# Squares of two layernorms moved from VectorE to ScalarE, with three other steps placed later

## The chip, the cores and the metric

One NeuronCore of a Trainium2 chip runs the whole program. The metric is the device time of one execution, in microseconds (us); lower is better.

## The reference, cut to what matters

```python
x = conv(x)                      # 8 x 56 x 56 x 64: 32 paths of 1x1, 3x3, 1x1 convs, summed, + x, relu
t = tokens(x)                    # 8 images of 3136 tokens, 64 channels
t = t + mamba(_ln_t(t))          # forward and backward selective scan, 128 channels, 16 states
t = t + ffn(_ln_t(t))            # 8 experts of 256, the best two of each token, mixed

def _ln_t(v, eps=1e-05):
    m = jnp.mean(v, axis=-1, keepdims=True)
    s = jnp.var(v, axis=-1, keepdims=True)
    return (v - m) / jnp.sqrt(s + eps)
```

The first lines are a summary; the mamba and the experts begin with a layernorm of their own. The kernel works in float32, or in bfloat16 parts that add up to it.

## The kernel before, in words

An image is cut in 7 chunks of 448 tokens (`CH`), each 4 tiles of 112 (`KT`, `TT`). The scan of one image takes 14 steps, one for each chunk and direction, with 16 slots each: 224 slots (`G`). In a slot `n`, TensorE picks the products for it (`pick_du`, L686, three matmuls into one of three banks), VectorE multiplies them by B (`weigh_b`, L1011, one slot ahead) and scans (`scan`, L1021), ScalarE makes the decays up to six slots ahead (`dA`, L864, in place in `dtb`, which a DMA spreads from DRAM), GpSimd multiplies by C (`by_c`, L1184), and TensorE gathers the result (L698). `pick_du` of slot n waits for the scan of slot n - 3.

Everything else is laid into these slots beside the scan. Stage A makes the next image's chunks: the convs, the first layernorm and its transposes. Stage E takes the finished chunks through the second layernorm, the router and the experts. Tables give each step its slot, relative to a chunk's start: `A_AT` (L62) and `E_AT` (L66). A chunk of A and one of E come every 32 slots, so the pattern repeats 56 times. Each engine has a loop over the slots and issues in order what the tables say. What follows counts slots within the 32, from the start of a chunk of E.

- **Norms.** `norm_mean` (L1058) sums the channels (L1059) and subtracts the mean (L1060, into `t[:, 0]`); `norm_var` (L1062) squares (L1063) and sums (L1064); `norm_pow` (L1066) divides by C (L1067), adds epsilon (L1068) and does three more small operations. All of it is on VectorE, each operation waiting for the one ahead. GpSimd raises to the power -1/2 (`power`, L1227; the operation is L1229) and writes the scaled tokens, twice. The first norm (tile `tmp`) is in slots 23 (mean) and 24 (the rest), the second (tile `tmpd`) in slots 0 and 1.
- **Ring.** Transposes and matmuls of A and E (`ring_job`) take two banks in turn; each waits until the bank's last content has been taken by ScalarE (`take`) or VectorE. The experts' first matmuls (`up`, L750) come in two bursts, two in each of the slots 24 to 27 and 0 to 3, and ScalarE takes them with Gelu (L906). `norm_T` (L739), `pair` (L760), `second` (L726, taken into h2p at L885) and `third` (L733) are ring jobs too.
- **Shared bank.** `misc_job` uses one bank for B (`bb`, L770), C (`cc`, L772), the next step's x and dt, and the tokens' transposes (`tokens_T`, L785). Each waits until the one ahead has been taken: B by `copy_bb` (L937), C by `copy_cc` (L943).
- **Mixing.** `down` (L821) gives a pair of experts, and `pair_out` (L1108) multiplies it on VectorE by the weights that ScalarE has put in `wb`, in slots 28, 31, 4 and 7. `wb` is the same tile as `rz`, into which ScalarE takes eight of the sixteen products of the convs' third stage (L895) from slot 8 on.
- **dt.** GpSimd makes dt (`soft_dt`, L1206) in slot 3 of a step; SP writes it (L537) and spreads it back over the partitions (L545).

Of the kernel before, what the change touches and what calls it, by code (L numbers as in the profile page):

```python
# [61 lines left out]
A_AT = {"cut": -16, "second": -11, "put0": -10, "rem1": -10, "split1": -7, "put1": -6, "rem2": -8,  # L62
        "split2": -5, "put2": -4, "arrange": -4, "z": 6, "x_in": 6, "paths": 14, "mean": 15, "var": 16,
        "power": 16, "scaled": 17, "normed": 18, "norm_T": 22, "keep_xn": 24}
F_AT = {"fetch": -4, "x_T": 0, "paths_in": 2, "rows": 4}
E_AT = {"mean": 0, "var": 1, "power": 2, "normed": 3, "tokens_T": 7, "logits": 10, "compare": 11, "places": 13,  # L66
        "lead": 13, "ask": 15, "weigh": 17, "share": 19, "weights": 20, "weight_parts": 21, "parts": 26,
# [13 lines left out]
def build(nc, T):  # L81
    ctx = ExitStack()
    with ctx:
# [5 lines left out]
        def sem(name):  # L89
            s = ctx.enter_context(nc.semaphore(name))  # L90
            sems.append(s)
            return s
# [275 lines left out]
        for s in sems:  # L368
# [11 lines left out]
            ("bu_ps", "bu_ok", "a_ok", "h_ok", "st_ok", "hc_ok", "y_acc", "gated", "o_ps", "o_rd", "st0"))  # L380
        v_ch, pw_req, pd_req = sem("v_ch"), sem("pw_req"), sem("pd_req")
        xa_in, rs_in = [sem("xa_in0"), sem("xa_in1")], [sem("rs_in0"), sem("rs_in1")]
        slab_in, h3_in, bounced = sem("slab_in"), sem("h3_in"), sem("bounced")
# [26 lines left out]
        def emit(p, run, a_imgs, e_imgs):  # L410
# [93 lines left out]
            for k in range(STEPS):  # L504
                if second_half(k):
                    MISC += [(DS * k + 4, "bb", k + 1), (DS * k + 5, "cc", k + 1)]
                if first_half(k):
                    MISC += [(DS * k + 12, "x", k + 2), (DS * k + 15, "dt", k + 2)]
# [23 lines left out]
            with nc.Block() as block:  # L532
# [318 lines left out]
                def _(act):  # L851
# [19 lines left out]
                    def take(what, of):  # L871
# [15 lines left out]
                        elif what == "third":  # L887
# [5 lines left out]
                            if m < 4:  # L893
                                after(ye_dve, earlier("E", "down", slots["A", "third", of]))
                            last = A.activation(rz[:, m % 4, :], out[:, 0:CH], ACT.Relu, bias=bnb[:, 2 + j:3 + j])  # L895
# [53 lines left out]
                    def keep_tokens(it):  # L949
                        act.wait_ge(m_ps, misc_made("tokens_T", it))  # L950
                        after(r_ps, made("up", (back(it, 2), MT - 1)))
                        A.activation(xn2[:, side(it), :], ps[MB][:, 0:CH], ACT.Copy).then_inc(m_act, 1)

                    def weigh(it):
                        act.wait_ge(e_req, upto("E", "ask", it))
                        A.activation(l1[:, 4, :], l1[:, 3, :], ACT.Exp).then_inc(e_ok, 1)  # L956
# [3 lines left out]
                    for n in range(SLOTS):  # L960
# [17 lines left out]
                        for a in (1, 2):  # L978
                            for it in now("A", ("", "split1", "split2")[a], n):
                                split_h2(it, a)  # L980
                        for it in now("E", "weigh", n):
                            weigh(it)
                        if k < STEPS:
                            if i == 5 and second_half(k):
                                copy_bb(k + 1)
                            if i == 6 and second_half(k):
                                copy_cc(k + 1)
                            if i == 15 and first_half(k):
                                soft_in(k + 2)

                @block.vector
                def _(dve):
# [64 lines left out]

                    def norm_mean(src, st, t):  # L1058
                        link(V.reduce_sum(st[:, 0, :], src, axis=AX.X))  # L1059
                        link(V.scalar_tensor_tensor(t[:, 0], bc_last(st[:, 0, :], C), -1.0 / C, src, ALU.mult, ALU.add))  # L1060

                    def norm_var(st, t):  # L1062
                        link(V.tensor_tensor(t[:, 1], t[:, 0], t[:, 0], ALU.mult))  # L1063
                        link(V.reduce_sum(st[:, 1, :], t[:, 1], axis=AX.X))  # L1064

                    def norm_pow(st, q, asked):  # L1066
                        link(V.tensor_scalar(st[:, 2, :], st[:, 1, :], 1.0 / C, None, ALU.mult))  # L1067
                        link(V.tensor_scalar(q[:, 0, 0, :], st[:, 2, :], LN_EPS, None, ALU.add))  # L1068
                        link(V.reciprocal(st[:, 3, :], q[:, 0, 0, :]))
                        link(V.tensor_tensor(st[:, 4, :], st[:, 2, :], st[:, 3, :], ALU.mult))  # L1070
                        V.tensor_scalar(q[:, 0, 1, :], st[:, 4, :], LN_EPS, None, ALU.add).then_inc(asked, 1)

                    def tokens_in(it):
# [3 lines left out]
                        after(d_tok, upto("E", "normed", back(it)))  # L1077
                        norm_mean(res_of(it, c), statd, tmpd)

# [42 lines left out]
                    for n in range(SLOTS):  # L1122
# [14 lines left out]
                        for it in now("A", "mean", n):  # L1137
                            norm_mean(res_of(it, A_ORD[it[1]]), stat, tmp)
                        for it in now("A", "var", n):
                            norm_var(stat, tmp)  # L1140
                            norm_pow(stat, pw, pw_req)
# [4 lines left out]
                        for it in now("E", "var", n):  # L1146
                            norm_var(statd, tmpd)
                            norm_pow(statd, pwd, pd_req)
# [264 lines left out]
```

## Time and profile before

| | |
|---|---|
| median of 3 runs | 5355.45 us (5351.28 to 5372.19) |
| the profiled execution | 5343.31 us |
| its span, first to last instruction | 5341.4 us |
| TensorE, VectorE, ScalarE, GpSimd busy | 83%, 78%, 62%, 74% |
| mean granted TensorE clock | 0.922 |

Busy time is the sum of the instructions on an engine. The ends of matmuls are modelled. "Waits" say for whom an engine stood idle and for how long; in the names, `ps` is a bank, and L numbers are lines of the kernel. PE is TensorE, DVE VectorE, ACT ScalarE and POOL GpSimd.

### The profile page before, as it was taken

To read this page: it belongs to the slowest core of one execution; us is meant where nothing else is said; L and a number is where in the kernel's file an instruction comes from. 1 tells how busy PE (TensorE), PEld (TensorE's weight loads), DVE (VectorE), ACT (ScalarE), POOL (GpSimd) and SP (SyncE) were. 2 spreads that over 40 slices of the span, in tenths; PEclk is the share of its full clock that TensorE was granted. 3 is DMA by queue.
4 is the path that set the end of the run, shared out by engine and by line. 5 is a ranking of instruction groups with operands and counts; after the bars stand their busy time and mean duration, and the time that the engine had idled before them with its cause. 6 is when DMAs were issued, how large, how long until landed. Compare 5 with 4: busy or idle time off the path is not lost. (4 is left out here: it accounts for less than half of the span.)

```text
span 5341.4 us, 71012 instructions
## 1 busy us (share of the span) xinstructions
PE 4435.6 (83%) x21206; PEld 1807.8 (34%) x21206; DVE 4141.3 (78%) x6297; ACT 3305.9 (62%) x5293; POOL 3949.6 (74%) x4937
## 2 busy tenths in 40 slices
PE   3577788888888888888888888788888888888887
PEld 1223333333333333333333333333333333332332
DVE  2278888788878887888878888788878888788871
ACT  1255466666666666666666666666666667666665
POOL 1267787778877877887878788778777778788872
PEclk9588899999999998999999999899999999999997
DMA  2365655555545554555555555455555555454420
GB/s 69 69 140 140 139 131 116 126 123 129 123 118 128 124 130 108 132 132 122 128 117 133 123 126 127 112 122 127 121 115 125 130 120 131 112 118 112 97 67 5
DMA packets 255561, 623.36 MB, mean 117 GB/s; under 512 B 105268, under 2 KB 170676, under 8 KB 255028
## 3 DMA queue, kind: packets, MB, share of 16 engines
q1 hardware_dynamic: 255156, 618.60, 50.2%
q8 instruction: 176, 2.88, 0.2%
q14 instruction: 229, 1.88, 0.1%
HBM read 540.85 MB, written 77.65 MB: 116 GB/s over the span
## 5 line engine op out<-in xcount | busy, mean ns | idle before, releaser
L1184 POOL TENSOR_TENSOR hc<-hs,cb 128x448 f32<-128x448 f32 x1792 | 2045.7, 1144 | 839.1 <-DVE hs L1021 810.3
L1021 DVE TENSOR_TENSOR_SCAN hs<-dtb,state,ps 128x448 f32<-128x448 f32 x1792 | 2049.0, 1143 | 110.2 <-DVE ps L1011 3.4
L1011 DVE TENSOR_TENSOR ps<-ps,bb 128x448 f32<-128x448 f32 x1792 | 1099.4, 614 | 508.8 <-PE ps L686 507.5
L686 PE MATMUL ps<-dux,pick 128*128 128x448 bf16 x3584 | 1066.3, 380 | 162.0 <-DVE hs L1021 99.7
L864 ACT ACTIVATE dtb<-dtb,decay 128x448 f32<-128x448 f32 x1792 | 1091.3, 658 | 95.7 <-DMA dtb<-dt_scratch 94.1
L906 ACT ACTIVATE hg<-ps,be 128x448 f32<-128x448 f32 x896 | 520.1, 631 | 576.9 <-PE ps L750 576.7
L686 PE MATMUL ps<-duz,pick 128*128 128x448 bf16 x1792 | 660.5, 369 | 0.0
L750 PE MATMUL ps<-xn,we 64*128 64x448 f32 x1792 | 578.2, 619 | 45.1 <-ACT hg L906 43.6
L895 ACT ACTIVATE rz<-ps,bnb 128x448 f32<-128x448 f32 x448 | 281.3, 628 | 476.3 <-DVE yw L1108 256.7
L686 PEld LDWEIGHTS ps<-dux,pick 128*128 128x128 bf16 x3584 | 273.1, 101 | 862.2 <-issue 444.3
L733 PE MATMUL ps<-h,w 96*128 96x448 bf16 x896 | 313.7, 385 | 219.6 <-ACT rz L895 82.3
L698 PE MATMUL ps<-hc,gather 128*32 128x448 f32 x3584 | 460.2, 587 | 5.4 <-POOL hc L1184 5.0
L821 PE MATMUL ps<-hg,we 128*64 128x448 f32 x1792 | 413.6, 585 | 18.0 <-ACT rz L913 7.0
L1044 DVE SCALAR_TENSOR_TENSOR acc<-ps,nb,acc 128x448 f32<-128x448 f32 x392 | 266.1, 679 | 189.3 <-PE ps L733 189.2
L810 PE MATMUL ps<-ident,rz 128*112 128x128 f32 x1792 | 297.2, 293 | 0.0
L975 ACT ACT_TABLE_LOAD x225 | 288.7, 1283 | 4.0
L750 PEld LDWEIGHTS ps<-xn,we 64*128 64x128 f32 x1792 | 199.4, 193 | 268.0 <-ACT hg L906 164.3
L810 PEld LDWEIGHTS ps<-ident,rz 128*112 128x112 f32 x1792 | 226.9, 142 | 157.6 <-issue 132.9
L686 PEld LDWEIGHTS ps<-duz,pick 128*128 128x128 bf16 x1792 | 179.1, 100 | 201.5 <-issue 34.2
L1282 POOL TENSOR_TENSOR yw<-yw 128x448 f32<-128x448 f32 x168 | 190.8, 1136 | 68.0 <-DVE yw L1108 68.0
L1225 POOL TENSOR_TENSOR h<-h,h2p 128x448 f32<-128x448 f32 x112 | 116.2, 1038 | 162.2 <-ACT h2p L885 104.3
L733 PEld LDWEIGHTS ps<-h,w 96*128 96x128 bf16 x896 | 84.0, 100 | 438.3 <-ACT rz L895 142.3
(177 smaller groups left out, 6426.5 us busy)
## 6 DMA issues: line engine op xcount, KB each, us to landing
dtb<-dt_scratch SPq DMA_DIRECT2D x448, 896.0 KB, 6.6
slab<-h_scratch SPq DMA_DIRECT2D x168, 290.0 KB, 8.1
dt_scratch<-sp SPq DMA_DIRECT2D x112, 224.0 KB, 2.0
h_scratch<-h2p SPq DMA_DIRECT2D x168, 112.0 KB
h<-h_scratch SPq DMA_DIRECT2D x56, 336.0 KB, 4.2
h_scratch<-h1s SPq DMA_DIRECT2D x56, 232.0 KB, 3.7
xw<-xn_scratch SPq DMA_DIRECT2D x112, 112.8 KB, 2.7
xw<-xn_scratch SPq DMA_DIRECT2D x112, 112.5 KB, 2.7
```

The source lines that it names most:

```text
L686: last = MM(ps[BU[n % 3]][:, 0:CH], pick[:, i, :], part, start=(a == 0), stop=(a == 2))
L698: last = MM(ps[YB][32 * q:32 * q + 32, 0:CH], gather[:, 24 - 8 * j:56 - 8 * j], hc[:, (4 * b + q) % 8, :], start=False, stop=(j == 3), ski ...
L733: last = MM(out[:, 0:CH], w3[:, j // 2, 2 * (j % 2):2 * (j % 2) + 2, :].rearrange("p a b -> p (a b)"), h3[:, j // 2, :], start=True, stop= ...
L750: last = MM(out[:, 0:CH], we1[half, m, :], xn2[half, side(it), :], start=True, stop=True)
L810: last = MM(ps[AB][0:TT, j * 128:(j + 1) * 128], src[:, j * TT:(j + 1) * TT], ident[:, :], is_transpose=True, start=(m == 0 and j == 0), s ...
L821: last = MM(ps[AB][C * h:C * h + C, 0:CH], we2[:, ORDER[g], :], hg[:, g % 8, :], start=(g % 4 < 2), stop=(g % 4 >= 2))
L864: A.activation(a, a, ACT.Exp, scale=decay[k % 2][:, i:i + 1]).then_inc(a_ok, 1)
L906: last = A.activation(hg[:, g % 8, :], out[:, 0:CH], ACT.Gelu, bias=be1[:, m:m + 1])
L975: A.preload_act_table_set("natural_log_exp_and_others")
L1011: V.tensor_tensor(bank, bank, bb[:, k % 2, :], ALU.mult).then_inc(bu_ok, 1)
L1021: V.tensor_tensor_scan(rev(hs[:, n % RH, :], d), rev(dtb[i // 4][:, i % 4, :], d), rev(bank, d), state[:, d, i:i + 1], ALU.mult, ALU.add). ...
L1184: P_.tensor_tensor(hc[:, n % 8, :], hs[:, n % RH, :], cb[:, k % 2, :], ALU.mult).then_inc(hc_ok, 1)
```

## The change

The square of both norms is computed by ScalarE (`square`), with the function Square and scale C^-0.5, so that the sum of the squares is the variance; the division by C is gone. VectorE signals the centred tokens (`x_mid`, `d_mid`), no longer waits for its own write of them, and waits for the squares (`x_sq`, `d_sq`) instead. The steps behind the mean come one slot later: variance, power, scaled, normed, `norm_T` and `keep_xn` of A; variance, power, normed and `tokens_T` of E. The product for C and its copy come one slot later. And a Relu of the third stage into `rz` no longer waits for all four pairs: the first waits for the first pair, the second for the second, and so on.

```diff
-        "split2": -5, "put2": -4, "arrange": -4, "z": 6, "x_in": 6, "paths": 14, "mean": 15, "var": 16,
-        "power": 16, "scaled": 17, "normed": 18, "norm_T": 22, "keep_xn": 24}
+        "split2": -5, "put2": -4, "arrange": -4, "z": 6, "x_in": 6, "paths": 14, "mean": 15, "square": 17, "var": 17,
+        "power": 17, "scaled": 18, "normed": 19, "norm_T": 23, "keep_xn": 25}
...
-E_AT = {"mean": 0, "var": 1, "power": 2, "normed": 3, "tokens_T": 7, "logits": 10, "compare": 11, "places": 13,
+E_AT = {"mean": 0, "square": 2, "var": 2, "power": 3, "normed": 4, "tokens_T": 8, "logits": 10, "compare": 11, "places": 13,
...
-                    MISC += [(DS * k + 4, "bb", k + 1), (DS * k + 5, "cc", k + 1)]
+                    MISC += [(DS * k + 4, "bb", k + 1), (DS * k + 6, "cc", k + 1)]
...
-                                after(ye_dve, earlier("E", "down", slots["A", "third", of]))
+                                after(ye_dve, earlier("E", "down", slots["A", "third", of]) - 3 + m)
...
+                    def square(t, centred, squared, count):
+                        act.wait_ge(centred, count)
+                        A.activation(t[:, 1], t[:, 0], ACT.Square, scale=C ** -0.5).then_inc(squared, 1)
...
+                        for it in now("A", "square", n):
+                            square(tmp, x_mid, x_sq, upto("A", "mean", it))
+                        for it in now("E", "square", n):
+                            square(tmpd, d_mid, d_sq, upto("E", "mean", it))
...
-                            if i == 6 and second_half(k):
+                            if i == 7 and second_half(k):
                                 copy_cc(k + 1)
...
-                    def norm_mean(src, st, t):
+                    def norm_mean(src, st, t, centred):
                         link(V.reduce_sum(st[:, 0, :], src, axis=AX.X))
-                        link(V.scalar_tensor_tensor(t[:, 0], bc_last(st[:, 0, :], C), -1.0 / C, src, ALU.mult, ALU.add))
-
-                    def norm_var(st, t):
-                        link(V.tensor_tensor(t[:, 1], t[:, 0], t[:, 0], ALU.mult))
-                        link(V.reduce_sum(st[:, 1, :], t[:, 1], axis=AX.X))
+                        V.scalar_tensor_tensor(t[:, 0], bc_last(st[:, 0, :], C), -1.0 / C, src, ALU.mult, ALU.add)\
+                            .then_inc(centred, 1)
+
+                    def norm_var(st, t, squared, count):
+                        dve.wait_ge(squared, count)
+                        link(V.reduce_sum(st[:, 2, :], t[:, 1], axis=AX.X))
...
-                        link(V.tensor_scalar(st[:, 2, :], st[:, 1, :], 1.0 / C, None, ALU.mult))
```

In the orders of the built programs, the lines of the changed kernel are one to nine higher than those above, by place. On ScalarE, at the burst of slots 0 to 3 (`hg` are the Gelus, `xns` the first norm's output, `sp` the steps of dt, `h2p` a split of the convs' second stage), before:

```order
L898 ACTIVATE xns<-ps,gb 128x448
L913 ACTIVATE rz<-ps 128x448
L926 ACTIVATE sp<-ps,dvec 128x448
L927 ACTIVATE sp<-ps,dvec 128x448
L929 ACTIVATE sp<-sp 128x448
L931 ACTIVATE sp<-sp 128x448
L906 ACT_TABLE_LOAD
L906 ACTIVATE hg<-ps,be 128x448 x4
L947 ACTIVATE h2p<-h 128x448
L906 ACTIVATE hg<-ps,be 128x448 x4
L975 ACT_TABLE_LOAD
```

and with the change, from the same place on:

```order
L927 ACTIVATE sp<-ps,dvec 128x448
L928 ACTIVATE sp<-ps,dvec 128x448
L930 ACTIVATE sp<-sp 128x448
L932 ACTIVATE sp<-sp 128x448
L899 ACTIVATE xns<-ps,gb 128x448
L907 ACT_TABLE_LOAD
L907 ACTIVATE hg<-ps,be 128x448 x4
L948 ACTIVATE h2p<-h 128x448
L907 ACTIVATE hg<-ps,be 128x448 x2
L957 ACTIVATE tmpd<-tmpd 112x256
L907 ACTIVATE hg<-ps,be 128x448 x2
L980 ACT_TABLE_LOAD
```

`xns` is now taken right ahead of the burst, and the Square (`tmpd<-tmpd`) stands behind the sixth of the eight Gelus; no table load comes with it, here or at the first norm, where it stands behind the fourth.

On TensorE from slot 5 on (`wcc` is the product for C, `wT,pick_w` a pair's weights, `pick` the products of a slot, `wo` the output projection, `xntd` the tokens' transposes, `hg,we` the experts' second matmul), before:

```order
L686 MATMUL ps<-duz,pick 128x448
L772 MATMUL ps<-u,wcc 128x448
L760 MATMUL ps<-wT,pick_w 128x448
L686 MATMUL ps<-dux,pick 128x448 x2
L686 MATMUL ps<-duz,pick 128x448
L705 MATMUL ps<-wo,zy 112x64 x4
L686 MATMUL ps<-dux,pick 128x448 x2
L686 MATMUL ps<-duz,pick 128x448
L785 MATMUL ps<-ident,xntd 128x112 x4
L821 MATMUL ps<-hg,we 64x448 x4
```

and with the change:

```order
L687 MATMUL ps<-duz,pick 128x448
L761 MATMUL ps<-wT,pick_w 128x448
L687 MATMUL ps<-dux,pick 128x448 x2
L687 MATMUL ps<-duz,pick 128x448
L773 MATMUL ps<-u,wcc 128x448
L706 MATMUL ps<-wo,zy 112x64 x4
L687 MATMUL ps<-dux,pick 128x448 x2
L687 MATMUL ps<-duz,pick 128x448
L822 MATMUL ps<-hg,we 64x448 x4
L687 MATMUL ps<-dux,pick 128x448 x2
L687 MATMUL ps<-duz,pick 128x448
L786 MATMUL ps<-ident,xntd 128x112 x4
```

C stands behind the pair's weights and the next slot's picked products, and the tokens' transposes behind the experts' matmul.

On TensorE from slot 28 on (`slab` is the convs' second stage, `xnt` the norm's transposes, `wdt` the product for dt), before:

```order
L726 MATMUL ps<-slab,w 32x448 x12
L686 MATMUL ps<-dux,pick 128x448 x2
L686 MATMUL ps<-duz,pick 128x448
L739 MATMUL ps<-ident,xnt 128x112 x4
L760 MATMUL ps<-wT,pick_w 128x448
L686 MATMUL ps<-dux,pick 128x448 x2
L686 MATMUL ps<-duz,pick 128x448
L781 MATMUL ps<-u,wdt 128x448
L698 MATMUL ps<-hc,gather 32x448 x4
L821 MATMUL ps<-hg,we 64x448 x4
```

and with the change:

```order
L727 MATMUL ps<-slab,w 32x448 x12
L687 MATMUL ps<-dux,pick 128x448 x2
L687 MATMUL ps<-duz,pick 128x448
L761 MATMUL ps<-wT,pick_w 128x448
L687 MATMUL ps<-dux,pick 128x448 x2
L687 MATMUL ps<-duz,pick 128x448
L782 MATMUL ps<-u,wdt 128x448
L740 MATMUL ps<-ident,xnt 128x112 x4
L699 MATMUL ps<-hc,gather 32x448 x4
L822 MATMUL ps<-hg,we 64x448 x4
```

The transposes of the norm stand behind the pair's weights and dt, where they stood ahead of both.

## Rows read from the trace of the kernel before

**Rows 1.** The page, part 1: busy us, share of the span, instructions of each engine.
```profile
PE 4435.6 (83%) x21206; PEld 1807.8 (34%) x21206; DVE 4141.3 (78%) x6297; ACT 3305.9 (62%) x5293; POOL 3949.6 (74%) x4937
```

**Rows 2.** Waits between engines: us in total, times, longest us.
```profile
ACT hg L906 <- PE ps L750: 576.7, 435, 4.9
DVE ps L1011 <- PE ps L686: 507.5, 428, 3.9
...
ACT rz L895 <- DVE yw L1108: 256.7, 45, 6.9
...
PE ps L772 <- ACT bb L937: 99.5, 55, 2.6
...
ACT dtb L864 <- DMA dtb<-dt_scratch: 94.1, 22, 9.4
...
PE ps L733 <- ACT rz L895: 82.3, 92, 2.3
...
PE ps L760 <- ACT h2p L885: 43.0, 45, 1.2
```

**Rows 3.** Timeline, first norm: start us, us, engine line op tiles, [idle before].
```profile
2611.33 0.57 PE L686 MATMUL ps<-dux,pick 128*128 128x448 bf16 x2 [1.02 <-DVE hs L1021]
...
2614.87 1.16 ACT L906 ACTIVATE hg<-ps,be 128x448 f32<-128x448 f32 x2 [0.64 <-PE ps L750]
...
2617.14 0.42 DVE L1060 SCALAR_TENSOR_TENSOR tmp<-stat,res 112x256 f32<-112x256 f32 x1
...
2618.81 1.16 ACT L906 ACTIVATE hg<-ps,be 128x448 f32<-128x448 f32 x2 [2.78 <-PE ps L750]
...
2624.18 0.57 PE L686 MATMUL ps<-dux,pick 128*128 128x448 bf16 x2
```

**Rows 4.** Groups of VectorE and GpSimd: busy us, mean ns | idle before.
```profile
L1229 POOL TENSOR_TENSOR pwd<-pwd,half_pow 112x8 f32<-112x8 f32 x56 | 92.9, 1659 | 13.0 <-DVE pwd L1071 13.0
...
L1063 DVE TENSOR_TENSOR tmp<-tmp 112x256 f32<-112x256 f32 x56 | 90.5, 1616 | 0.0
...
L1063 DVE TENSOR_TENSOR tmpd<-tmpd 112x256 f32<-112x256 f32 x56 | 59.1, 1055 | 0.0
...
L1067 DVE TENSOR_SCALAR stat<-stat 112x4 f32<-112x4 f32 x56 | 32.0, 571 | 1.9
...
L1067 DVE TENSOR_SCALAR statd<-statd 112x4 f32<-112x4 f32 x56 | 26.4, 471 | 1.9
...
L1068 DVE TENSOR_SCALAR pw<-stat 112x4 f32<-112x4 f32 x56 | 9.5, 170 | 1.9
```

**Rows 5.** One line, L1063: duration ns minimum/median/maximum, first and last start.
```profile
L1063 DVE TENSOR_TENSOR tmp<-tmp x56: 415/1809/1819, 138.4 to 4766.0; 112x256 f32<-112x256 f32 x56
```

**Rows 6.** Timeline, second norm and the burst beside it.
```profile
2553.10 0.63 DVE L1011 TENSOR_TENSOR ps<-ps,bb 128x448 f32<-128x448 f32 x1 [2.07 <-PE ps L686]
...
2554.05 1.16 ACT L906 ACTIVATE hg<-ps,be 128x448 f32<-128x448 f32 x2 [0.50 <-PE ps L750]
...
2555.89 0.62 DVE L1060 SCALAR_TENSOR_TENSOR tmpd<-statd,res 112x256 f32<-112x256 f32 x1
...
2559.69 1.16 ACT L906 ACTIVATE hg<-ps,be 128x448 f32<-128x448 f32 x2 [0.58 <-PE ps L750]
```

**Rows 7.** Groups of ScalarE, nearest in kind to a Square.
```profile
L947 ACT ACTIVATE h2p<-h 128x448 bf16<-128x448 f32 x112 | 64.0, 572 | 11.2 <-POOL h L1225 10.5
...
L956 ACT ACTIVATE l<-l 112x4 f32<-112x4 f32 x56 | 11.0, 197 | 7.8 <-DVE l L1095 7.7
```

**Rows 8.** Timeline, the shared bank between B and C.
```profile
2566.43 0.52 ACT L937 ACTIVATE bb<-ps 128x448 f32<-128x448 f32 x1
...
2567.00 1.42 PE L772 MATMUL ps<-u,wcc 128*128 128x448 f32 x2 [1.86 <-ACT bb L937]
```

**Rows 9.** Timeline, TensorE at the conv's third stage.
```profile
2581.13 0.36 PE L733 MATMUL ps<-h,w 96*128 96x448 bf16 x1 [0.49 <-ACT rz L895]
```

**Rows 10.** Timeline, TensorE at the pair's weights.
```profile
2634.16 0.36 PE L760 MATMUL ps<-wT,pick_w 24*128 24x448 bf16 x1 [1.19 <-ACT h2p L885]
```

More of the change, by code:

```diff
@@ L381, in build @@
         v_ch, pw_req, pd_req = sem("v_ch"), sem("pw_req"), sem("pd_req")
+        x_mid, x_sq, d_mid, d_sq = (sem(n) for n in ("x_mid", "x_sq", "d_mid", "d_sq"))
         xa_in, rs_in = [sem("xa_in0"), sem("xa_in1")], [sem("rs_in0"), sem("rs_in1")]
@@ L1077, in tokens_in @@
                         after(d_tok, upto("E", "normed", back(it)))
-                        norm_mean(res_of(it, c), statd, tmpd)
+                        norm_mean(res_of(it, c), statd, tmpd, d_mid)
                     def scores(it):
@@ L1137, in _ @@
                         for it in now("A", "mean", n):
-                            norm_mean(res_of(it, A_ORD[it[1]]), stat, tmp)
+                            norm_mean(res_of(it, A_ORD[it[1]]), stat, tmp, x_mid)
                         for it in now("A", "var", n):
-                            norm_var(stat, tmp)
+                            norm_var(stat, tmp, x_sq, upto("A", "square", it))
                             norm_pow(stat, pw, pw_req)
@@ L1146, in _ @@
                         for it in now("E", "var", n):
-                            norm_var(statd, tmpd)
+                            norm_var(statd, tmpd, d_sq, upto("E", "square", it))
                             norm_pow(statd, pwd, pd_req)
```

## The prediction

> **What bounds the kernel now.** I read the busy shares first [rows 1]: no engine is full. TensorE leads with 83%, but a matmul's end is modelled, so this is no proof; VectorE has 78%. The waits between engines come next [rows 2], since they tell who keeps whom. VectorE stands 507.5 us for the picked products (L1011 behind L686) and ScalarE 576.7 us for the experts' matmuls (L906 behind L750), and TensorE stands for ScalarE at three places: 99.5 us before L772, 82.3 us before L733, 43.0 us before L760. So the lead goes round, and each part of the change has to be read in its own slots. One chunk takes 32 slots. The timelines are those of one chunk in the middle of the run, which repeats 56 times (7 chunks, 8 images).
>
> Around the first layernorm the chain goes so. TensorE first stands at L686 for a scan [rows 3], so it is there as far ahead of VectorE as its three banks allow. In the next microseconds VectorE does the mean (L1060) and then, a slot later, the square. But behind that square TensorE's L686 at 2624.18 carries no wait for the scan: by then TensorE and ScalarE have become the late ones, in the burst of Gelu.
>
> **The squares.** Off VectorE go L1063 (90.5 and 59.1 us) and L1067 (32.0 and 26.4 us) [rows 4]: 208.0 us busy. The reduction and the small operations stay. L1063 takes 415 ns at its fastest and 1809 ns in the median, both for the same 112x256 [rows 5], so most of it is waiting for something that GpSimd holds, not arithmetic. L1067 looks alike: 571 ns for four elements, where the next operation (L1068) takes 170. The square leaves and that wait goes with it, but the wait of L1067 may simply move to L1068, which is the same kind of operation behind the same reduction. So VectorE's busy time falls by 149.6 us plus 19 (112 times 0.17) to 58.4 us, to about 3.93 to 3.97 ms. The Trainium skill (SBUF — State Buffer, section "SBUF: two separate sides") says that VectorE and GpSimd share one port pair, and that "the shared pair is an exclusive lock": the loser waits for the whole instruction of the other. By that rule L1068 inherits the wait of L1067, so the lower of the two cuts is the right one.
>
> How much of it is on the path? Between nothing (it was all in VectorE's slack) and all 208 us. Rows 3 speak for nearly nothing at the first norm, since TensorE does not wait behind it. At the second, VectorE had just waited 2.07 us for TensorE [rows 6]. I take 0.1 us a chunk, 6 us.
>
> ScalarE gains 112 squares of 112x256. No Square stands in the trace. The nearest rows are 197 ns for four elements a partition (L956) and 572 ns for 448 (L947) [rows 7]; on the line between them 256 elements cost 0.41 us, in all 46 us of an engine that is 62% busy. Do they push the Gelus behind them? First norm: the burst's fourth Gelu ends at 2616.03, the mean ends at 2617.56, the square would end at about 2618.0, and the next Gelu starts only at 2618.81 [rows 3]. There is 0.8 us to spare, and TensorE cannot come further ahead of VectorE there. Second norm: the mean is ready at 2556.51; the square falls between Gelus that have 0.58 us of idle time between them [rows 6], against 0.41. Cost: nothing, bounded by 0.41 us for each of 112 (46 us) if TensorE gains on ScalarE in the burst and the cover goes. VectorE's new wait for the square stands behind a scan and a product of the next slot, 1.8 us, longer than the square: nothing. What stands behind that wait is the scan, on which GpSimd and TensorE hang, so if it ever waits it is dear. No table load is added: the built programs have the same number on ScalarE, and the square stands inside the burst with no load around it.
>
> The Trainium skill (ScalarE: Activation LUTs, section "Rules for kernel authors") speaks against this part: a multiplication belongs on VectorE. By it the sum would lose these 6 us and take ScalarE's 46 us in, if ScalarE had no room. The rows here have the VectorE square at 1616 and 1055 ns in the mean, more than the estimate for ScalarE.
>
> **The product for C, one slot later.** In slot 4 ScalarE empties the shared bank (L937 ends at 2566.97) and TensorE, which wants it for L772, stands 1.86 us [rows 8]. Now a pair's product L760 and the next three L686 come first. These are 0.36 and about 0.9 us, from 2565.14 on, so 1.2 us of the wait is covered and 0.6 us stays. Of 99.5 us in 55 places [rows 2] I count 1.2 x 55 = 66 us. Bounds: 0, if the work pulled ahead only waits later, and the whole 99.5.
>
> **The wait for the mixing, loosened.** The first Relu of the conv's third stage (L895) waits for the last pair's product on VectorE (L1108): 256.7 us in 45 places [rows 2], 5.7 us each. It now waits for the first pair's, long done. ScalarE's idle time is not the gain: right behind it stand L864, which need the spread of dt from a DMA (94.1 us of waits already, [rows 2]), so that DMA is late next. GpSimd now makes dt before the power of the second norm, 1.66 us earlier (L1229) [rows 4], which gives that DMA some room. The gain is what TensorE waited for these Relus: 0.49 us in the chunk shown [rows 9], of 82.3 us in all [rows 2]. I take 0.5 x 56 = 28 us, bounds 0 and 82.3.
>
> **Transposes of the norm, one slot later.** TensorE waits 1.19 us at L760 for h2p [rows 10], because L739 has taken the bank between. With L739 behind, L760 needs no bank of the second stage. But ScalarE is nearly full there, and only its own 0.50 us before the next Gelus can be won [rows 6]: 0.5 x 56 = 28 us, bounds 0 and 43.0. The other delays of a slot (the power, the scaled tokens, the store of xn, the tokens' transposes) fall on results wanted two slots later or more; SP's store of xn now stands behind a dt spread that is already released: nothing.
>
> **The sum.** 6 + 66 + 28 + 28 = 128 us. The profiled execution had 5343.31 us (span 5341.4), so 5215 by it. The median of the runs shown is 12 us above it, 5355.45; against that the sum gives **5227 us**, 2.4% faster. All times below are against the median. A difference under 0.5% (27 us) can't be told from none in this kernel.
>
> **Rivals.**
> *Half of it.* The three waits sit on engines that meet again half a chunk later; if the gains overlap (ScalarE's DMA sets L733 whatever TensorE won at L772), about half stays: 5291. For it: the 94.1 us on the DMA. Chance 0.15.
> *The waits only change hands.* bb is late since ScalarE has six L864 to do after the burst, and no placement makes it earlier. If ScalarE is the chain throughout, only some 15 us go: 5340. Against it: ScalarE's 576.7 and 256.7 us of idle time. Chance 0.13.
> *VectorE was the bound.* TensorE does stand 1.02 us for it [rows 3]. If the whole cut reaches the end alone, 5355 - 208 = 5147; with the placements too, 5019. Against it: no wait behind the square. Chance 0.16.
> *Slower: the square stalls the Gelu burst.* ScalarE executes in order, so if it reaches the first square before the mean is written, it stands 1.53 us (2616.03 to 2617.56) and 0.41 us more, with the Gelus behind it, and through two banks TensorE. This is free up to 0.8 us and dear beyond. If the placements bring the expert matmuls forward by more than that, the price is 1.94 us less no cover, 56 times, and 0.41 at the second norm: 109 + 23 = 132 us, 5487. Against it: TensorE already waits for a scan there, so its lead is full. Chance 0.06.
> *The change doesn't do what it says* (loads of tables around the squares, or work back in its old order): the order of the built program excludes it.
>
> **How the numbers follow.** The forecast has the remaining 0.50. Range 5140 to 5350: it holds the forecast with its smaller bounds, the half, nearly all of the change of hands, and the start of VectorE's case (5147); outside are the slower case and the part of VectorE's case below 5140, together about 0.17. Faster by over 0.5%: 0.50 + 0.15 + 0.16 = 0.81, of which I give 0.01 away for the loosest bounds: 0.80. Within 0.5%: 0.13. Slower: 0.07.
>
> **What would show it.** VectorE's busy time 3.93 to 3.97 ms, with the operation that was L1068 at about 570 instead of 170 ns if the wait moves to it. A Square of 0.41 us, 112 of them, and no more table loads. The wait before the successor of L772 down from 99.5 to about 35 us; that of L760 for h2p gone; ScalarE's wait for the mixing gone, and a larger one for the DMA in its place. VectorE's waits for L686 do not fall much, since the time off VectorE becomes waiting: they stay near 507.5 us or grow. I am wrong if ScalarE shows a wait for the mean that delays the Gelus, or if the three waits go and the span does not shorten.

## The result and the profile after

The changed kernel takes 5215.6 us (median of four runs, 5207.0 to 5225.7) against 5358.6 us for the kernel before on the same chip: ratio 0.9728, interval 0.9703 to 0.9753. The forecast was 5227 us in a range of 5140 to 5350. The total is right; most terms of the sum are not, as the experiments show.

The lines have moved by one to ten: L686 is L687, L750 L751, L760 L761, L772 L773, L864 L865, L1011 L1020, L1021 L1030, L1184 L1193. The square is L957 on ScalarE, and the operations behind the reduction (L1068 to L1071 before) are L1077 to L1080. The page, part 1, of the changed kernel, as [rows 1] for before:

```profile
PE 4357.3 (84%) x21206; PEld 1771.7 (34%) x21206; DVE 4025.3 (77%) x6073; ACT 3334.8 (64%) x5405; POOL 3922.9 (75%) x4937
```

VectorE lost 4141.3 - 4025.3 = 116.0 us of busy time, not the 168 to 208 foreseen. TensorE lost 78.3 us with the very same 21206 matmuls, which nothing in the prediction provides for: its clock was granted higher (0.937 in the mean of this profiled execution, 0.922 before).

Waits between engines in the changed kernel (us in total, times, longest us), to be held against [rows 2]:

```profile
POOL hc L1193 <- DVE hs L1030: 726.9, 463, 16.0
...
DVE ps L1020 <- PE ps L687: 437.9, 398, 6.6
ACT hg L907 <- PE ps L751: 429.0, 396, 6.8
...
ACT dtb L865 <- DMA dtb<-dt_scratch: 193.5, 57, 6.5
...
ACT tmp L957 <- DVE tmp L1069: 119.2, 56, 9.3
...
PE ps L734 <- ACT rz L896: 86.3, 84, 3.7
...
PE ps L786 <- POOL xntd L1243: 62.8, 46, 5.0
...
PE ps L773 <- ACT bb L938: 41.2, 46, 1.7
```

The wait for C went from 99.5 to 41.2 us (forecast: about 35). The wait at L760 for h2p (43.0) and ScalarE's wait for the mixing (256.7) have no row left. In the place of the latter ScalarE waits 193.5 instead of 94.1 us for the DMA that spreads dt, as foreseen, but TensorE's own wait for these Relus did not fall at all: 86.3 against 82.3 us. And there are 62.8 us for the scaled tokens of the second norm, a wait that the prediction costed at nothing (its row before is 20.1 us). VectorE's wait for picked products, which was to stay near 507.5 us or grow, fell to 437.9.

The first norm, timeline of the changed kernel (start us, us, engine line, [idle before]), as [rows 3]:

```profile
2551.26 0.42 ACT L957 ACTIVATE tmp<-tmp 112x256 f32<-112x256 f32 x1 [1.55 <-DVE tmp L1069]
...
2552.49 1.16 ACT L907 ACTIVATE hg<-ps,be 128x448 f32<-128x448 f32 x2 [0.81 <-PE ps L751]
...
2554.46 2.22 POOL L1193 TENSOR_TENSOR hc<-hs,cb 128x448 f32<-128x448 f32 x2
2554.52 0.41 DVE L1074 TENSOR_REDUCE stat<-tmp 112x4 f32<-112x256 f32 x1
2554.96 1.75 DVE L1077 TENSOR_SCALAR pw<-stat 112x4 f32<-112x4 f32 x1
```

ScalarE stands 1.55 us in front of the square for the mean, almost the 1.53 us of the slower rival, and the Gelus behind it still wait for TensorE (0.81 us): the cover held. Four elements a partition take VectorE 1.75 us, and they end at 2556.71, within 0.03 us of GpSimd's pair of products (2556.68). The two products take 1.13 us each, so VectorE stood through the rest of the first and the whole of the second.

Groups of VectorE and ScalarE in the changed kernel (busy us, mean ns | idle before), as [rows 4]:

```profile
L1077 DVE TENSOR_SCALAR pw<-stat 112x4 f32<-112x4 f32 x56 | 82.3, 1471 | 1.9
...
L1077 DVE TENSOR_SCALAR pwd<-statd 112x4 f32<-112x4 f32 x56 | 18.6, 332 | 1.9
...
L957 ACT ACTIVATE tmp<-tmp 112x256 f32<-112x256 f32 x56 | 23.3, 417 | 119.2 <-DVE tmp L1069 119.2
L957 ACT ACTIVATE tmpd<-tmpd 112x256 f32<-112x256 f32 x56 | 23.3, 416 | 2.1 <-DVE tmpd L1069 2.1
```

And the first of these lines by itself (duration ns minimum/median/maximum), beside [rows 5]:

```profile
L1077 DVE TENSOR_SCALAR pw<-stat x56: 169/1735/1747, 141.9 to 4639.7; 112x4 f32<-112x4 f32 x56
```

So the square of the first norm was 1616 ns in the mean because it stood where GpSimd is busy, and what stands there now inherits the wait: L1068 took 170 ns, its successor L1077 takes 1471. The 90.5 us taken off with L1063 came back as 82.3 - 9.5 = 72.8 us. (With the steps a slot later and the square still on VectorE, L1063 is even slower, 1991 ns, and L1068 stays at 170.) The Square costs 0.417 us, 112 times, 46.6 us, as estimated (0.41 and 46).

### The profile page after: what moved, and what is told of

Read it like the earlier page. It is cut to its first block and busy times, and to the rows that moved or that the text cites. A ratio compares the mean times of both kernels' runs of the same rounds, so it can differ in the third digit from the quotient of the medians.

```text
span 5211.8 us, 70837 instructions
## 1 busy us (share of the span) xinstructions
PE 4357.3 (84%) x21206; PEld 1771.7 (34%) x21206; DVE 4025.3 (77%) x6073; ACT 3334.8 (64%) x5405; POOL 3922.9 (75%) x4937
## 5 line engine op out<-in xcount | busy, mean ns | idle before, releaser
L1193 POOL TENSOR_TENSOR hc<-hs,cb 128x448 f32<-128x448 f32 x1792 | 2030.5, 1136 | 751.6 <-DVE hs L1030 726.9
L1030 DVE TENSOR_TENSOR_SCAN hs<-dtb,state,ps 128x448 f32<-128x448 f32 x1792 | 2047.4, 1143 | 105.8 <-issue 1.8
L1020 DVE TENSOR_TENSOR ps<-ps,bb 128x448 f32<-128x448 f32 x1792 | 1098.7, 613 | 443.9 <-PE ps L687 437.9
L865 ACT ACTIVATE dtb<-dtb,decay 128x448 f32<-128x448 f32 x1792 | 1086.2, 657 | 198.4 <-DMA dtb<-dt_scratch 193.5
L687 PE MATMUL ps<-dux,pick 128*128 128x448 bf16 x3584 | 1049.1, 374 | 164.6 <-DVE hs L1030 102.5
L687 PE MATMUL ps<-duz,pick 128*128 128x448 bf16 x1792 | 649.2, 362 | 0.0
L751 PE MATMUL ps<-xn,we 64*128 64x448 f32 x1792 | 583.3, 621 | 53.5 <-ACT hg L907 53.0
L687 PEld LDWEIGHTS ps<-dux,pick 128*128 128x128 bf16 x3584 | 264.6, 99 | 865.4 <-issue 527.8
L734 PE MATMUL ps<-h,w 96*128 96x448 bf16 x896 | 313.0, 385 | 212.5 <-ACT rz L896 86.3
L822 PE MATMUL ps<-hg,we 128*64 128x448 f32 x1792 | 401.4, 570 | 18.4 <-ACT rz L914 7.5
L751 PEld LDWEIGHTS ps<-xn,we 64*128 64x128 f32 x1792 | 203.6, 194 | 273.0 <-ACT hg L907 173.8
L687 PEld LDWEIGHTS ps<-duz,pick 128*128 128x128 bf16 x1792 | 176.9, 99 | 195.6 <-issue 23.3
L734 PEld LDWEIGHTS ps<-h,w 96*128 96x128 bf16 x896 | 83.8, 101 | 419.9 <-ACT rz L896 153.6
```

The costliest lines, as they stand in the source:

```text
L687: last = MM(ps[BU[n % 3]][:, 0:CH], pick[:, i, :], part, start=(a == 0), stop=(a == 2))
L734: last = MM(out[:, 0:CH], w3[:, j // 2, 2 * (j % 2):2 * (j % 2) + 2, :].rearrange("p a b -> p (a b)"), h3[:, j // 2, :], start=True, stop= ...
L751: last = MM(out[:, 0:CH], we1[half, m, :], xn2[half, side(it), :], start=True, stop=True)
L822: last = MM(ps[AB][C * h:C * h + C, 0:CH], we2[:, ORDER[g], :], hg[:, g % 8, :], start=(g % 4 < 2), stop=(g % 4 >= 2))
L865: A.activation(a, a, ACT.Exp, scale=decay[k % 2][:, i:i + 1]).then_inc(a_ok, 1)
L1020: V.tensor_tensor(bank, bank, bb[:, k % 2, :], ALU.mult).then_inc(bu_ok, 1)
```

## The experiments

There were twelve runs of eleven kernels (the placements twice, the changed kernel once more), in three groups, each beside the kernel before on the same chip (its medians: 5361.0, 5363.9 and 5365.6 us). "Late norm steps" means the table entries of the change for var, power, scaled, normed, norm_T, keep_xn and tokens_T.

**All the placements, squares left on VectorE.** The kernel before with:

```diff
-"var": 16, "power": 16, "scaled": 17, "normed": 18, "norm_T": 22, "keep_xn": 24   (A_AT)
+"var": 17, "power": 17, "scaled": 18, "normed": 19, "norm_T": 23, "keep_xn": 25
-"var": 1, "power": 2, "normed": 3, "tokens_T": 7                                  (E_AT)
+"var": 2, "power": 3, "normed": 4, "tokens_T": 8
-(DS * k + 5, "cc", k + 1)         if i == 6 and second_half(k):
+(DS * k + 6, "cc", k + 1)         if i == 7 and second_half(k):
-after(ye_dve, earlier("E", "down", slots["A", "third", of]))
+after(ye_dve, earlier("E", "down", slots["A", "third", of]) - 3 + m)
```

> The kernel before with every placement of the change (norm steps a slot later, C a slot later, the loosened wait), but with the squares and the division by C left on VectorE. My theory (the placements are the gain, the squares lie in VectorE's slack and only cost 6 us or less to keep): 5359 - 122 = about 5237 us, at most 0.5% above the changed kernel's 5215.6. Rival (the squares were the gain): 5320 us or more. The variance with its own square stands in slots 25 and 2; VectorE then should not wait less than before for L686 after the first norm.

Measured: 5204.3 us, ratio 0.9696 (0.9661 to 0.9731). Without the squares' move the kernel is at least as fast as the changed one. So both kernels ran again, on one chip.

> The placements without the squares on ScalarE, once more: 5204 us; the same as the changed kernel within 0.3% if the squares lie off the path, 1% slower than it if they are part of the gain.

> The changed kernel once more, on the chip of its three neighbours here, so that the squares' own price can be read: about 5216 us. With the squares left on VectorE (placements) the time was 5204.3; my theory now is that the squares give nothing or cost up to 0.2% (11 us), since TensorE waits as long for scans either way and ScalarE stands 1.5 us for the mean. Rival (they gain, and the two jobs' chips differed): this kernel comes out below that of the placements.

Measured: 5197.5 us, 0.9683 (0.9663 to 0.9702), for the placements alone; 5218.9 us, 0.9723 (0.9705 to 0.9742), for the changed kernel. The intervals don't meet, if only just; the five times are 5180 to 5209 and 5202 to 5225 us. Moving the squares **costs** 0.4% here, 21 us. Where it goes is in the waits of the first of the two placements runs (us in total, times, longest us):

```profile
POOL hc L1184 <- DVE hs L1021: 668.3, 448, 15.6
...
DVE ps L1011 <- PE ps L686: 339.3, 267, 6.6
ACT dtb L864 <- DMA dtb<-dt_scratch: 220.4, 59, 8.7
...
PE ps L733 <- ACT rz L895: 72.7, 66, 3.4
```

and its page, part 1:

```profile
PE 4353.6 (83%) x21206; PEld 1770.4 (34%) x21206; DVE 4113.5 (79%) x6297; ACT 3296.0 (63%) x5293; POOL 3941.3 (76%) x4937
```

The squares' move takes 4113.5 - 4025.3 = 88.2 us of work off VectorE, and VectorE's wait for picked products rises from 339.3 to 437.9, by 98.6 us. (The second pair, on one chip, has 83.2 us less work and 106.3 us more waiting.) What it was relieved of became waiting, entirely, and TensorE waits 86.3 instead of 72.7 us before L734. So the part of the change that gives it its name gives nothing; the placements are the change.

**The changed kernel with C and the mixing wait as before.** Its two edits undone:

```diff
-(DS * k + 6, "cc", k + 1)         if i == 7 and second_half(k):
+(DS * k + 5, "cc", k + 1)         if i == 6 and second_half(k):
-after(ye_dve, earlier("E", "down", slots["A", "third", of]) - 3 + m)
+after(ye_dve, earlier("E", "down", slots["A", "third", of]))
```

> Squares on ScalarE with the norm steps a slot later (norm_T and tokens_T too), but C in its old slot and the mixing wait as it was. My theory: the C term of 66 us and the 28 us of the mixing are missing, 5359 - 6 - 28 = about 5325 us. Rival (the gain is in the norms' part): 5260 us or less. The wait before the product for C should be about 99 us again, as before.

Measured: 5247.5 us, 0.9783 (0.9746 to 0.982). Most of the gain is still there: a miss of 78 us for the working of the prediction, by which 94 of 128 us should have gone. The wait before the product for C is 99.7 us, as expected.

**Only the transposes of the norm and the store one slot later.**

```diff
-"norm_T": 22, "keep_xn": 24
+"norm_T": 23, "keep_xn": 25
```

> The kernel before with the transposes of the first norm and the store of xn one slot later, nothing else. My theory: 0.5 us a chunk, 5359 - 28 = about 5331 us. The slots from 28 to 31 were 0.97 us shorter a chunk in the changed kernel, so a second reading says 54 us, 5305 us. Rival (ScalarE is full there): no change, 5359.

Measured: 5269.9 us, 0.983 (0.9798 to 0.9862): 91 us, where the prediction had 28. The timeline of this kernel at the pair's weights, to be held against [rows 10]:

```profile
2596.17 3.47 ACT L864 ACTIVATE dtb<-dtb,decay 128x448 f32<-128x448 f32 x6
...
2600.11 0.36 PE L760 MATMUL ps<-wT,pick_w 24*128 24x448 bf16 x1 [0.21 <-ACT rz L913]
...
2605.72 1.28 ACT L906 ACT_TABLE_LOAD   x1
...
2607.02 1.16 ACT L906 ACTIVATE hg<-ps,be 128x448 f32<-128x448 f32 x2
```

The same stretch in the kernel before:

```profile
2628.43 3.47 ACT L864 ACTIVATE dtb<-dtb,decay 128x448 f32<-128x448 f32 x6
...
2636.00 0.64 ACT L926 ACTIVATE sp<-ps,dvec 128x448 f32<-128x448 f32 x1 [0.29 <-PE ps L781]
...
2638.40 1.28 ACT L906 ACT_TABLE_LOAD   x1
...
2640.18 1.16 ACT L906 ACTIVATE hg<-ps,be 128x448 f32<-128x448 f32 x2 [0.50 <-PE ps L750]
```

Counted from the six L864, L760 starts at 3.94 instead of 5.73 us, the table load at 9.55 instead of 9.97, and the first Gelus at 10.85 instead of 11.75: 0.90 us earlier, 50 us in 56 chunks. The prediction had allowed only the last 0.50 us, since it took ScalarE for nearly full; but ScalarE had small waits for TensorE ahead of the burst as well (0.29 us at L926), and they went too. The other 41 us I look for further down, at the clock; they are not fully explained.

**Only C one slot later.**

```diff
-(DS * k + 5, "cc", k + 1)         if i == 6 and second_half(k):
+(DS * k + 6, "cc", k + 1)         if i == 7 and second_half(k):
```

> The kernel before with the product for C and its copy one slot later, nothing else. My theory: 1.2 us a chunk, 5359 - 66 = about 5293 us, and the wait before L772 falls from 99.5 to about 35 us. Rival (the work pulled ahead only waits later): 5345 us or more with the wait gone all the same.

Measured: 5306.6 us, 0.9909 (0.9878 to 0.994), 54 us against 66 foreseen. Its wait row:

```profile
PE ps L785 <- POOL xntd L1234: 86.6, 50, 3.7
...
PE ps L772 <- ACT bb L937: 40.4, 45, 1.7
```

99.5 - 40.4 = 59 us of wait went, and 54 us of time. But the first row was 20.1 us before: TensorE now comes sooner to the tokens' transposes (L785) and stands 66.5 us more for GpSimd there. By its waits it has won nothing, as the rival says; by the clock it has (further down).

**Only the mixing wait loosened.**

```diff
-after(ye_dve, earlier("E", "down", slots["A", "third", of]))
+after(ye_dve, earlier("E", "down", slots["A", "third", of]) - 3 + m)
```

> The kernel before with only the loosened wait for the mixing. My term was 28 us: about 5333. Rival (a DMA takes the place of the wait, and TensorE waits for the Relus as before): 5355 to 5361 us, with ScalarE's wait for VectorE's product (256.7 us) gone and its wait for the spread of dt grown from 94 us to 200 or more.

Measured: 5331.5 us, 0.9924 (0.9903 to 0.9946), 32 us against 28 foreseen; its six executions lie widely apart, 5302 to 5354 us. The rows of its profiled execution, the slowest of them:

```profile
ACT dtb L864 <- DMA dtb<-dt_scratch: 180.3, 53, 9.5
...
PE ps L733 <- ACT rz L895: 57.8, 54, 2.7
```

Alone, this edit does what the prediction says: ScalarE's 256.7 us of waiting become only 86 us more for the DMA, and TensorE gains 82.3 - 57.8 = 24.5 us.

**These three together**, the other late norm steps in their old slots (the last three edits above in one kernel).

> The kernel before with only norm_T (and the store of xn) and C a slot later and the loosened wait; the variances, powers and tokens stay in their old slots. norm_T alone gave 91 us and C alone 54 us. Theory one (the terms add, the norms' own slots are worth nothing): 5361 - 145 = about 5216 us. Theory two (the later variance of the second norm is worth 0.9 us a chunk in slots 0 to 4, lost again at the tokens): 5216 to 5240. If it comes below 5200 the later norm steps cost time.

Measured: 5246.6 us, 0.9776 (0.9761 to 0.9792), 117 us, where the single kernels add up to 91 + 54 + 32 = 177. And it is 49 us slower than the placements kernel on the same chip, which differs from it only in var, power, scaled, normed and tokens_T one slot later: the steps costed at nothing are worth 49 us. (In the mean of 42 chunks slots 0 to 3 take 12.56 us here and 11.83 in the placements kernel.)

**Only the late norm steps**, squares on VectorE, C and the mixing wait as before (the first four lines of the first diff).

> The kernel before with the norms' steps behind the mean one slot later (variance, power, scaled, normed, norm_T, store, tokens' transposes) and nothing else. norm_T alone gave 91 us; with C and the loosened wait the norms' other steps were worth another 49 us (three_only against placements). Theory (terms overlap, the other steps are worth something only with room made by the others): 5240 to 5275. Rival (they add): 5225 or less.

Measured: 5257.8 us, 0.9806 (0.9778 to 0.9833), against 0.983 for the transposes and the store alone: these intervals overlap, so without C and the loosened wait the other late steps are worth nothing that can be told. Beside 0.9783 for the same kernel with the squares moved (on another chip) the intervals overlap, so in that surrounding the squares cost nothing that can be told.

**One square at a time.** The changed kernel with the second norm, and then with the first, given back its square on VectorE:

```diff
-for it in now("E", "square", n):
-    square(tmpd, d_mid, d_sq, upto("E", "mean", it))
...
+link(V.tensor_tensor(t[:, 1], t[:, 0], t[:, 0], ALU.mult))
+link(V.reduce_sum(st[:, 1, :], t[:, 1], axis=AX.X))
+link(V.tensor_scalar(st[:, 2, :], st[:, 1, :], 1.0 / C, None, ALU.mult))
```

> The changed kernel with only the first norm's square on ScalarE; the second norm squares and divides on VectorE, in the slots of the change. The placements without squares gave 5197 to 5204 us, the changed kernel 5216 to 5219. Theory (both squares give their time back at the next wait for a product, and cost a little): 5205 to 5212, half of the difference. Rival (only the first costs, since ScalarE stands 1.5 us in the burst for the mean): 5216 to 5219, as the changed kernel.

> The changed kernel with only the second norm's square on ScalarE. Theory: 5205 to 5212 us. Rival (the first is the only dear one): 5197 to 5204, as the placements alone. If both kernels equal the placements within 0.2%, the difference of the two squares is not more than the scatter.

Measured: 5225.9 us, 0.9747 (0.9721 to 0.9773), with only the first on ScalarE; 5234.7 us, 0.9761 (0.9733 to 0.9788), with only the second. Both misses: I expected at least one half to lie between the changed kernel and the placements. Neither does. Both are at or above the whole change (0.9723 and 0.9728) and clearly above the placements.

These two runs can't price a square, though. I took the time from one scan on VectorE to the next as the length of a slot, in images 1 to 6 (42 chunks), and give the mean of a chunk in us:

| slots | placements (second run) | changed (again) | only the first | only the second |
|---|---|---|---|---|
| 0 to 3 | 11.83 | 11.09 | 11.80 | 11.04 |
| 4 to 11 | 21.12 | 22.01 | 20.78 | 21.95 |
| 12 to 15 | 11.80 | 11.88 | 11.61 | 11.86 |
| 16 to 23 | 18.31 | 18.21 | 18.90 | 18.81 |
| 24 to 31 | 23.41 | 23.71 | 23.85 | 23.51 |
| all | 86.47 | 86.90 | 86.94 | 87.18 |

With the second norm's square on ScalarE, slots 0 to 3 are some 0.75 us shorter, and slots 4 to 11 some 0.9 us longer: the relief does arrive, and is lost again behind it. But the two halves also lose 0.5 to 0.7 us in slots 16 to 23, where no square stands, 28 to 39 us in 56 chunks and more than the difference in question. It sits in 9 and in 6 of the 42 chunks, which take 21 to 22 us there. In one of them, of the kernel with only the first on ScalarE:

```profile
2387.01 1.15 DVE L1028 TENSOR_TENSOR_SCAN hs<-dtb,state,ps 128x448 f32<-128x448 f32 x1 [0.35 <-issue]
...
2396.45 2.56 DVE L1067 SCALAR_TENSOR_TENSOR tmp<-stat,res 112x256 f32<-112x256 f32 x1
```

VectorE starts a scan 0.35 us late without a wait that the profile shows, and four slots on the subtraction of the first norm's mean (L1067) takes 2.56 us, where it takes 0.42 in a chunk without that delay. Why these two programs have it stays open, and with it how the 21 us divide between the norms. The half with only the first has VectorE's L1084 (the successor of L1068) at a mean of 1248 ns, the other has it at 170: the inherited wait belongs to the first norm, as read above.

**The placements kernel with the second norm's scaled tokens back in slot 3**, to take away the 62.8 to 70.0 us that TensorE waits for them:

```diff
-"power": 3, "normed": 4
+"power": 3, "normed": 3
```

> The placements without the squares on ScalarE, but the second norm's scaled tokens in slot 3, right behind the power, and not in slot 4 behind the first product of dt. TensorE then should not wait for them before the tokens' transposes (70 us in the placements, 46 times). If that wait is on the path: 5197 - 40 to 70 = 5130 to 5160 us. Rival (the wait moves to dt, whose products now come 2 us later on GpSimd): 5200 or more.

Measured: 5264.6 us, 0.9821 (0.9794 to 0.9847), over 60 us slower than the placements. The wait for the tokens did go. TensorE at slots 8 to 11 of this kernel:

```profile
2451.45 0.41 PE L733 MATMUL ps<-h,w 96*128 96x448 bf16 x1 [1.98 <-ACT rz L895]
```

its waits:

```profile
ACT dtb L864 <- DMA dtb<-dt_scratch: 300.4, 59, 8.9
...
PE ps L733 <- ACT rz L895: 143.6, 86, 3.6
```

and the clock around it (stretch, us, PE busy, granted clock, DMA share, GB/s):

```profile
2449.00:2450.50 1.50, 0.47 (x3) 1.00 1.09 229
2450.50:2452.00 1.50, 0.55 (x2) 0.88 1.05 231
2452.00:2453.50 1.50, 1.50 (x2) 0.50 0.75 120
2453.50:2455.00 1.50, 1.50 (x9) 0.50 0.80 215
2455.00:2456.50 1.50, 1.50 (x8) 0.50 1.02 225
```

The work arrives 1.8 us earlier (slots 4 to 7 take 8.5 instead of 10.3 us in one chunk) only to meet a transfer that doesn't come earlier. ScalarE then stands for the DMA, TensorE stands 1.98 us in one piece, and behind that the clock is granted at half. Slots 8 to 11 take 15.2 us here against 10.1 in the placements kernel.

That chunk shows what the clock costs. ScalarE at the transfer, here and in the placements kernel:

```profile
2449.65 1.23 ACT L864 ACTIVATE dtb<-dtb,decay 128x448 f32<-128x448 f32 x2 [4.82 <-DMA dtb<-dt_scratch]
```

```profile
2426.50 1.23 ACT L864 ACTIVATE dtb<-dtb,decay 128x448 f32<-128x448 f32 x2 [2.99 <-DMA dtb<-dt_scratch]
```

and slots 8 to 11 of both as one stretch (us; busy of PE, PEld, DVE, ACT, POOL; granted clock, DMA share, GB/s):

```profile
2444.70:2459.90 15.20, 13.10 (x50) 4.93 (x50) 9.04 (x15) 5.12 (x9) 13.02 (x18) 0.78 0.89 194
```

```profile
2423.40:2433.50 10.10, 9.84 (x50) 4.03 (x50) 8.99 (x14) 5.07 (x9) 10.10 (x12) 1.00 0.75 163
```

Counted from slot 0 (2425.2 here, 2402.1 there), L864 starts at 24.45 and 24.40 us: up to there nothing is lost. Behind it the chunk loses 15.2 - 10.1 - 1.8 = 3.3 us. The same 50 matmuls are busy 3.3 us longer, and 15.2 us at a clock of 0.78 are 3.3 us of lost clock. In this chunk the loss is the clock's, as far as these rows can tell.

## The clock behind the waits

The same view, of the kernel before, where TensorE stands 1.86 us before L772:

```profile
2475.50:2477.00 1.50, 0.83 (x5) 1.00 0.20 62
2477.00:2478.50 1.50, 0.30 (x1) 1.00 0.75 196
2478.50:2480.00 1.50, 1.50 (x4) 0.58 1.08 201
2480.00:2481.50 1.50, 1.50 (x7) 0.50 0.41 100
2481.50:2483.00 1.50, 1.50 (x9) 0.50 0.32 120
2483.00:2484.50 1.50, 1.50 (x9) 0.50 0.44 162
```

TensorE had been idle for much of two stretches (0.83 and 0.30 of 1.50 us busy), and then ran at 1.2 instead of 2.4 GHz for most of the 6 us of the last four rows. The slots 4 to 7 of that chunk as one stretch, first before, then with only C moved (us; busy of PE, PEld, DVE, ACT, POOL; granted clock, DMA share, GB/s):

```profile
2476.90:2488.60 11.70, 10.19 (x37) 4.87 (x37) 8.21 (x12) 5.00 (x10) 11.46 (x14) 0.71 0.76 181
```

```profile
2457.20:2467.10 9.90, 6.70 (x36) 3.00 (x34) 8.09 (x12) 4.93 (x10) 9.66 (x13) 1.00 0.67 159
```

Yet in that same stretch of the latter kernel TensorE stands as long, at another place:

```profile
2462.96 0.57 PE L785 MATMUL ps<-ident,xntd 112*128 112x112 f32 x4 [2.06 <-POOL xntd L1234]
```

I worked the loss out for every slot of images 1 to 6 (42 chunks): its length times (1 - granted clock), the mean of a chunk in us.

| kernel | slots 5 to 7 | slot 11 | all 32 |
|---|---|---|---|
| before | 1.82 | 0.12 | 5.25 |
| transposes and store later | 0.93 | 0.12 | 3.82 |
| C later | 0.24 | 0.43 | 3.68 |
| mixing wait loosened | 2.39 | 0.07 | 6.25 |
| these three | 0.48 | 0.37 | 3.74 |
| placements (second run) | 0.04 | 0.36 | 3.21 |
| changed | 0.00 | 0.60 | 3.55 |
| placements, tokens in slot 3 | 0.00 | 2.13 | 4.87 |

Each row is one execution, and the clock scatters: the kernel before has 0.908 to 0.924 in the 30 executions beside the experiments, and 0.922 in the profiled one. That scatter alone is worth about 1.4 us a chunk, so small differences in this table say little. In the mean of all executions the clock is 0.914 for the kernel before on two of the chips, and on the same chips 0.917 with the mixing wait loosened, 0.933 with C and with the transposes later, 0.935 with these three, 0.936 changed and 0.941 for the placements (second run); with the tokens in slot 3 it is 0.926, beside 0.918 for the kernel before on that third chip. So the mixing wait, whose row looks worse than the kernel before, is no worse by these means.

The change won 1.70 us of clock a chunk, 95 us in 56, if all of it had been on the path; it isn't, since some of those slots would wait anyway. For the last row against the placements it is 1.66 us a chunk, 93 us, where the medians differ by 67. It also says why single gains don't add: transposes, C, and the three together each end near 3.7 to 3.8, so a recovery is counted twice if they are added (over all 32 slots 1.43 and 1.57 us a chunk, 80 and 88 us, against 1.51 for both with the third; in slots 5 to 7 0.89 and 1.58, against 1.34). That the clock accounts for the overlap is argued from these rows; no run held the clock fixed, so its share stays open.

## Why the prediction was right, and where it was not

**The total** came out 11 us from the forecast because misses of both signs cancelled, and that is luck. By the experiments the sum is 177 us for the three placements alone, less 60 that they share, and 49 for the other late steps, less 21 for the squares: 145 us. Measured are 143, and the forecast had 128.

- *Squares, a gain of 6 us:* wrong in sign. On one chip they cost 21 us. "Nothing for ScalarE" held: 1.55 us in front of the square, and the Gelus behind it still waited for TensorE in the chunk shown; ScalarE is idle again right behind the square in 52 of the 56 places. What failed is the step before it: I took VectorE's relief for worth nothing to slightly positive, and the relief was waited away in full (88.2 us less work, 98.6 us more waiting). By slots, the second norm's relief comes in slots 0 to 3 and is lost in 4 to 11. Why the balance is negative stays open.
- *VectorE's busy time, 3.93 to 3.97 ms:* 4.025. I let a wait move to L1068 that L1067 had (571 ns), but not the larger one of L1063. The wait doesn't belong to the operation but to its place beside GpSimd's work. The Trainium skill (SBUF — State Buffer, section "SBUF: two separate sides") says that the loser waits for the other's whole instruction; by that rule an operation that needs the port in that place waits whatever its size, and the trace agrees (1735 ns in the median for four elements). It shows more: the wait spans the rest of one of GpSimd's products and the whole of the next. I had cited the rule and applied it to one of two operations.
- *C one slot later, 66 us:* 54 alone, but not on the path foreseen. The wait at L772 fell by 59, with 60 foreseen; in its place TensorE's wait for the tokens (L785) rose from 20.1 to 86.6 us, which I had not seen coming, so TensorE waited no less. What the kernel won stands in slots 4 to 7, 11.06 us a chunk before and 10.13 with C moved, where the clock is granted higher (the loss in slots 5 to 7 fell from 1.82 to 0.24 us). That the number came near is luck.
- *Mixing wait, 28 us:* 32 alone, TensorE's own share 24.5 in the profiled execution. Right by itself, within its scatter. In the whole change TensorE's wait there is 86.3 against 82.3 us, so it was given back, to the DMA that I had named as late next.
- *Transposes one slot later, 28 us:* 91 alone, and the step that failed most. The bound of 43.0 us was TensorE's wait at L760 and no bound on the gain: a product that comes 1.79 us earlier also ends waits of others behind it (0.90 us at the Gelus). Less clock is lost in slots 5 to 7 of this kernel too (0.93 instead of 1.82 us); that the one leads to the other is not shown.
- *Other late steps, nothing:* 49 us on top of the three, and nothing that can be told without C and the mixing wait. I had looked only at whether their results came too late, not at what they made way for. The wait for the tokens (62.8 us) doesn't come from them: it is 86.6 us with only C moved, 83.4 with the three, 70.0 with the late steps added to these, and 13.8 with the late steps only. Taking it away by an earlier slot made the kernel slower.
- *The sum of terms:* 177 us alone, 117 together. I added them as if independent, though the rival "half of it" said that they overlap.

Of the rivals, "VectorE was the bound" falls with the placements kernel. "Slower: the square stalls the Gelu burst" had its 1.5 us right, and its cover held. "The waits only change hands" is true of the squares, of C, and of the mixing wait within the whole, but not of the change.

**The better version** is the kernel before with the placements and its own squares: 5204.3 and 5197.5 us, 0.9696 and 0.9683 of the time before, 0.4% under the changed kernel.

## What to carry to other kernels

When an operation is far slower than its fastest instance, ask what it waits for before moving it: if the wait belongs to the place, the next operation inherits it, and relief of an engine that is ahead turns into waiting. Where a change is a bundle, run the bundle without the part that names it. Add up all waits of an engine, and not only the one that you meant to shorten. And cost a wait of TensorE not only by its own length but by the clock that follows it: look at the granted clock of the stretch behind each long wait, and don't add gains that recover the same stretch.

## What the runs showed of the hardware that I had not expected

- A TENSOR_SCALAR of four elements a partition took 169 ns at its fastest and 1735 ns in the median, beside two products on GpSimd of 1.13 us each, ending 0.03 us behind the second (in 46 of 56 places).
- The reduction of 256 elements just ahead of it took 409 ns in the median and 420 at most, beside the same products: it is not held.
- Behind a stand of TensorE of 1.86 or 1.98 us the granted clock was 0.50 to 0.58 for 6 us in the one place, and 0.50 in the three rows after it in the other. Not every such stand does it: the kernel with only C later stands 2.06 us before L785 in the same chunk, and slots 4 to 7 have a clock of 1.00. What decides is not settled here.
- The matmuls' busy time fell from 4435.6 to 4357.3 us with their number unchanged. By the mean clock alone it would be 4435.6 x 0.922 / 0.937 = 4365 us, most of the fall.
